# A fused graph layer on one core: VectorE's order between the first and the second group, and three gate matmuls moved

## The reference

```python
h = jnp.maximum(_layernorm(x, axis=-1), 0.0)
# inside the layer, with x standing for h:
c = relu(bn1(conv1d(xc, conv1_w, 0)))                 # 1 tap, along the channels
c = bn2(conv1d(c, conv2_w, 8))                        # 17 taps, along the nodes
x_conv = relu(c + xc)
s = x @ w_se.T + b_se                                 # 3 numbers per node
A = exp(-dist(s, s)) * mask
x_nmp = A @ relu(x @ w_msg.T + b_msg)
gi = concat([x_conv, x_nmp]) @ w_ih.T + b_ih          # gates r, z, n
gh = x @ w_hh.T + b_hh
r, z = sigmoid(gi_r + gh_r), sigmoid(gi_z + gh_z)
nn_ = tanh(gi_n + r * gh_n)
return (1 - z) * nn_ + z * x
```

## Time and profile before

| | |
|---|---|
| median of 3 runs | 283.03 us (282.77 to 283.75) |
| profiled execution | 282.48 us, of which span of the instructions 280.7 us |
| granted TensorE clock, mean | 0.998 |
| PE busy | 273.1 us, 97% |
| DVE busy | 244.4 us, 87% |
| ACT busy | 162.0 us, 58% |
| POOL busy | 63.3 us, 23% |

### The profile page before, as it was taken

The page is one execution under the profiler, slowest core; times in us unless marked ns, Lnnn a source line. Parts: engine busy times, 40 slices in busy tenths (PEclk is TensorE's granted clock), DMA queues, the critical chain, the costliest instruction groups (busy, mean ns, idle before and its releaser), DMA issues.

```text
span 280.7 us, 5274 instructions
## 1 busy us (share of the span) xinstructions
PE 273.1 (97%) x1842; PEld 246.4 (88%) x1842; DVE 244.4 (87%) x550; ACT 162.0 (58%) x270; POOL 63.3 (23%) x125
## 2 busy tenths in 40 slices
PE   7899999999999999999999999999999999999993
PEld 6699977999889988899889998899889998899883
DVE  6899988998999999988999989988999887984656
ACT  3798558737654657526754467536674267542463
POOL 7600020920225002610216002530116100340000
PEclk9999999999999999999999999999999999999999
DMA  7830405656243654182542743263440712043002
GB/s 229 304 43 0 147 6 154 223 117 183 77 152 56 149 198 138 42 132 81 218 152 39 166 152 112 113 95 112 152 152 7 124 54 96 2 61 70 0 0 75
DMA packets 20029, 30.77 MB, mean 110 GB/s; under 512 B 9458, under 2 KB 13876, under 8 KB 19124
## 3 DMA queue, kind: packets, MB, share of 16 engines
q1 hardware_dynamic: 17312, 26.50, 28.6%
q0 software_dynamic: 2544, 3.93, 10.2%
q10 hardware_dynamic: 148, 0.01, 0.0%
HBM read 25.41 MB, written 8.70 MB: 122 GB/s over the span
## 4 chain that ended last, share of the span: by engine, by line
PE 87%; DVE 5%; DMA 2%; ACT 2%; issue 1%; POOL 1%; SPq 0%; DVEq 0%; ACTq 0%; POOLq 0%
PE ps L1311 24%; PE ps L1313 23%; PE ps L1312 23%; PE ps L1364 5%; PE ps L1401 4%; DMA w<-w_conv 2%; PE ps L1424 2%; PE ps L1430 1%; PE ps L1433 1%; PE ps L1391 1%; ACT cp L544 1%; POOL rstd L408 1%; DVE stats L827 1%; DVE n_lo L1031 0%; PE ps L1360 0%
## 5 line engine op out<-in xcount | busy, mean ns | idle before, releaser
L1311 PE MATMUL ps<-v_hi,wt_hi 128*128 128x256 f32 x280 | 79.3, 283 | 0.0
L1313 PE MATMUL ps<-v_hi,wt_lo 128*128 128x256 f32 x280 | 78.8, 282 | 0.0
L1312 PE MATMUL ps<-v_lo,wt_hi 128*128 128x256 f32 x280 | 78.7, 281 | 0.0
L1311 PEld LDWEIGHTS ps<-v_hi,wt_hi 128*128 128x128 f32 x280 | 52.7, 188 | 0.8
L1312 PEld LDWEIGHTS ps<-v_lo,wt_hi 128*128 128x128 f32 x280 | 52.6, 188 | 0.3
L1313 PEld LDWEIGHTS ps<-v_hi,wt_lo 128*128 128x128 f32 x280 | 52.7, 188 | 0.0
L581 ACT ACTIVATE mbs<-ps,par 128x256 f32<-128x256 f32 x24 | 12.0, 501 | 30.7 <-DVE y L970 17.6
L414 POOL TENSOR_TENSOR scale<-vpe,neg_half 128x8 f32<-128x8 f32 x6 | 10.2, 1695 | 83.3 <-DVE scale L844 83.3
L1311 PE MATMUL ps<-h_hi,wt_hi 128*128 128x512 f32 (+1 forms) x67 | 26.7, 398 | 0.5 <-DVE h_lo L879 0.3
L1312 PE MATMUL ps<-h_lo,wt_hi 128*128 128x512 f32 (+1 forms) x67 | 25.7, 384 | 0.0
L1313 PE MATMUL ps<-h_hi,wt_lo 128*128 128x512 f32 (+1 forms) x67 | 25.7, 384 | 0.0
(11 more groups left out here) (167 smaller groups left out, 642.3 us busy)
## 6 DMA issues: line engine op xcount, KB each, us to landing
w<-ln_rows SPq DMA_DIRECT2D x6, 1024.0 KB, 4.7
mask<-adj_t SPq DMA_DIRECT2D x8, 512.0 KB, 3.5
out<-x_t SPq DMA_DIRECT2D x7, 512.0 KB, 5.4
out<-gate POOLq DMA_DIRECT2D x14, 256.0 KB, 4.1
xin<-x_nm SPq DMA_DIRECT2D x6, 512.0 KB, 3.7
xt<-x_t SPq DMA_DIRECT2D x6, 512.0 KB, 4.3
slot_rows<-turned SPq DMA_DIRECT2D x24, 32.0 KB, 3.2
rows<-slot_rows SPq DMA_DIRECT2D x6, 128.0 KB, 3.0
```

Of the source, the lines that this page charges most:

```text
L1311: pe.matmul(dst, wt_hi[:, blk, :], hi, start=start, stop=False)
L1312: pe.matmul(dst, wt_hi[:, blk, :], lo, start=False, stop=False)
L1313: return pe.matmul(dst, wt_lo[:, blk, :], hi, start=False, stop=stop)
```

## The change

On DVE, `ln_stats` takes a range of tiles, and for group 1 it is called twice, for tiles 0 to 3 ahead of the two `n_low` (and now behind `lot_low(12)`) and for tiles 4 to 7 behind them. `update` is cut into `change` (L1074, L1077) and `put_out` (L1081); for group 0, half 0, the two `h_low` of group 1 stand between them. `moments(2)` moves from in front of `level2_b(1, 0)` to behind `v_low_b(1, 1)`. On PE, `gates_xc` is cut into `xc_reset` (three matmuls, reset gate) and `xc_rest` (six), and for group 0, half 1, `xc_reset` stands ahead of `messages(1)`. All other calls give the same instructions in the same order as before. The diff, with the split of `update` left to the words above:

```diff
-            def ln_stats(g):
+            def ln_stats(g, tiles=range(GB)):
 
                 dve.wait_ge(x_landed, 16 * (g + 1))
-                for j in range(GB):
+                for j in tiles:
                     last = stats_of(g, j)
-                last.then_inc(stats_ready, 1)
+                if j == GB - 1:
+                    last.then_inc(stats_ready, 1)
...
             add_shared(0, 1)
-            ln_stats(1)
             lot_low(12)
+            ln_stats(1, range(0, 4))
             n_low(0, 0, 5)
             n_low(0, 1, 7)
+            ln_stats(1, range(4, GB))
             join_y(0, 1, 0)
             join_y(0, 1, 1)
...
             reset(0, 0)
-            update(0, 0)
+            change(0, 0)
             h_low(1, 0)
             h_low(1, 1)
+            put_out(0, 0)
             ln_stats(2)
-            moments(2)
             level2_b(1, 0)
             level2_b(1, 1)
             level1(1)
             v_low_b(1, 0)
             v_low_b(1, 1)
+            moments(2)
             level2_u(1)
...
+            def xc_reset(g, c):
+                pe.wait_ge(xc_lo_ready, NCH * g + c + 1)
+                three(bank(4), IH(R, 0), xc_hi[:, cols(c)], xc_lo[:, cols(c)], False, True).then_inc(r_ps, 1)
...
             conv1(1, 0, 2)
             conv1(1, 1, 7)
+            xc_reset(0, 1)
             messages(1)
-            gates_xc(0, 1)
+            xc_rest(0, 1)
```

More of the change, by code:

```diff
@@ L1069, in slots_low_first, with change @@
                 dve.tensor_tensor(left[:, :, 13], sq[:], left[:, :, 12], ALU.subtract).then_inc(slot_lo, 1)
-            def update(g, c):
+            def change(g, c):
                 dve.wait_ge(cand_ready, NCH * g + c + 1)
@@ L1078, in update, with put_out @@
                                          op1=ALU.mult).then_inc(zd_ready, 1)
+            def put_out(g, c):
                 dve.wait_ge(zd_ready, NCH * g + c + 1)
@@ L1082, in update @@
                                          op1=ALU.add).then_inc(out_ready, 1)
+            def update(g, c):
+                change(g, c)
+                put_out(g, c)
             def part_scaled(p):
@@ L1501, in gates_n, with xc_rest @@
                 three(bank(6), IH(Z, 1), *nm, False, False)
-            def gates_xc(g, c):
+            def xc_reset(g, c):
+                pe.wait_ge(xc_lo_ready, NCH * g + c + 1)
+                three(bank(4), IH(R, 0), xc_hi[:, cols(c)], xc_lo[:, cols(c)], False, True).then_inc(r_ps, 1)
+            def xc_rest(g, c):
                 xc = (xc_hi[:, cols(c)], xc_lo[:, cols(c)])
[L1505 to L1513, removed]
                 if g < NG - 1:
@@ L1519, in gates_xc @@
                     three(bank(5), IH(N, 0), *xc, False, True).then_inc(gin_ps, 1)
+            def gates_xc(g, c):
+                if n_last(g, c):
+                    xc = (xc_hi[:, cols(c)], xc_lo[:, cols(c)])
+                    pe.wait_ge(xc_lo_ready, NCH * g + c + 1)
+                    three(bank(4), IH(R, 0), *xc, False, False)
+                    pe.wait_ge(n_lo_ready, NCH * g + 1)
+                    three(bank(5), IH(N, 0), *xc, True, False)
+                    three(bank(6), IH(Z, 0), *xc, False, False)
+                    return
+                xc_reset(g, c)
+                xc_rest(g, c)
             def part_n_of_h(p):
```

## The result

The changed kernel takes 287.22 us (median of 4 executions, 284.49 to 287.45), the kernel before 283.3 beside it; the ratio is 1.0127, with a 95% interval of 1.0093 to 1.0161. The forecast was 284.7 in a range of 283.3 to 285.9: the direction and the first cause were right, the size was not.

What follows compares the result with a forecast made beforehand. PE was taken as the bound, busy 97% of the span, plus its holes. The early 0.67 us gain is spent waiting for slots: 282.48 + 1.67 = 284.15, plus 0.55 to the median's scale, 284.7 us; range 283.3 to 285.9.

Steps and rivals of the forecast that it cites:

- the first cause: DVE's late moments delays POOL's scale, then distances and the slots; PE's transposes wait, 1.67 us later than before.
- First part: DVE: group 1 statistics in halves about n_low end PE's stall at 35.88; xc still starts at 38.05, worth nothing.
- n stall: PE's short stall at 35.88 for n's low parts, 0.20 us in the timeline, counted as worth 0.45.
- Second and third part: DVE's h_low inside update, PE's reset matmuls before messages: two stalls hidden, first sub-convolution at 51.4, gain 0.67 us.
- The sum: Whole execution: profiled 282.48 us plus 1.67 for late slots gives 284.15, or 284.7 on the median's scale.
- Fourth part: DVE's moments at 50.95 makes POOL's distances 3.07 us later, slots ready at 58.55, PE's transposes 1.67 us later.
- the cap of 0.64: POOL beside DVE's L970: if cover never cost over 0.64 us, slots at 58.15 and time 284.3; judged unlikely.
- no row prices it: TensorE's clock in PE's 2.3 us hole: no earlier PE wait near that long, so no cost was given.
- Rival (d): PE's hole of 2.3 us: equal or more contention, or TensorE's clock lowered; 286 us and above, chance 0.08.
- behind it nothing is late: After PE's wait for slots: rows, exponent, masks and joins move with PE, column-row transfers stay hidden; no further cost.
- The base: Starting time: median of runs 283.03 us, taken as 0.55 above the profiled execution of 282.48.

Runs made afterwards that it cites:

- `reset_only`: Only the reset gate's three xc matmuls moved ahead of messages, against the kernel before: median 283.39 us, ratio 0.998 [0.9937, 1.0023].

## Where the prediction held, and the step that failed

- **First part, right.** The n stall is gone, xc starts at 37.90 (the whole execution lies 0.15 earlier from the start), and the weight load's wait before it has grown from 0.25 to 0.73 (PEld, 37.90 in the profile after); alone this part is worth nothing.
- **Second and third part, right and a little better.** No stall at 45.15 and 47.23. The first sub-convolution comes at 51.00, not 51.4: messages' copies on ScalarE end at 50.94, since messages is not only earlier but also starts with its weight load covered. A gain of 0.92 us (1.07 less the 0.15), against my 0.67. The sum had left it out, rightly: it is spent in the wait for the slots.
- **Fourth part, the mechanism right, the size near by some luck.** Moments at 50.58 (I said 50.95), distances at 53.67 (53.77), slots at 58.86 (58.55), PE 1.88 late (1.67). L414 took 1.97 instead of 1.69, which made up for most of the early moments. I took one operation left when DVE's add_h begins, and 59.15 for two; there were two, L291 and L293, and add_h began 0.31 us earlier than I placed it (56.97, not 57.28). 59.15 less 0.31 is 58.84. The open point, whether POOL can be covered for the whole length of a long DVE operation, is settled by L291, 1.21 us beside L971: the cap of 0.64 is refuted. The Trainium skill ("SBUF — State Buffer", SBUF: two separate sides) has it so, and this trace agrees.
- **The step that failed: the clock's fall stands in the sum as nothing, because "no row prices it".** I had said that PE would stand for 2.3 us where it had no hole. Rival (d) named what could follow, with 0.08 for it and for more contention together, and the sum went on as if the clock held. The runs show it in 8 of the 12 executions of the changed kernel without the transfer wait, at 1.5 us each, and in 8 of the 9 of the changed kernel as it is. It is true that ahead of PE's last matmuls the trace before has no stretch below 1.00, so neither the chance of a fall nor its length could be read there. But I had the rate, half the work per us, and the trace after bears it out: a matmul of 256 columns every 0.22 us against 0.12. With a mean of 0.57 over 4 us, 0.43 of them is lost, 1.7 us, near the 1.5 measured. A state that the trace has never been in needs a term with a range, and a chance to match, not a footnote.
- **A second step failed: "behind it nothing is late".** I followed rows, masks and column rows of the group at hand, and not the same chain in the groups behind. In group 5 the distances of the changed kernel wait 1.31 us for the rows of the slots. In the experiments this wait costs 1.4 us.
- **The base.** I took the median (283.03) as the profiled execution plus 0.55 of no cause. By the experiments it was a mixture: executions near 282.5 and others with a wait of PE in group 5 that the profiled one did not have. SP's chain of stores and loads there was not looked at, since nothing in it was changed. The profiled execution plus 1.9 is 284.4, and that is where the undisturbed executions lie (284.38 to 284.50).

That the transfer wait is there in eight of the nine executions of the changed kernel is read from their times; two profiles show it. Why it goes with the fall of the clock there, and is absent in all ten executions with the filled hole, is open.

## What to carry to other kernels

An instruction moved on one engine moves everything that is queued behind its consumers on other engines: here `moments`, ten small operations, held up eleven of another purpose, which came second in POOL's loop. Before moving a step, read each consumer's queue in program order and ask what stands behind it and how much slack that has (here 0.5 us against 3 us). And where a sum says that a hitherto busy TensorE will stand for two us, give the clock a term of its own. Dummy matmuls in the hole are a remedy while the cause of the hole stays: here it then cost its length and no more.

## What the runs showed of the hardware beyond the forecast

The granted clock fell to its lower level behind holes of 2.69 us and 1.87 us; in other executions it did not behind 1.31, 1.89 or 1.99 us, nor, by their times and mean clocks, in 4 of 12 behind the hole of 2.7 us. The fall behind the hole of 2.7 us cost 1.5 us. POOL operations on 8 and 16 elements a partition that took 0.22 and 0.20 us took 1.21 and 1.10 us beside a DVE operation of 1.22 us on two operands in SBUF; beside operations that read PSUM, POOL's operations took 0.20 to 0.28. In group 5 SP's first load of the rows follows its first store by 7.0 to 7.3 us in the profiled executions with the wait and by 5.0 to 5.4 in those without (7.2 in one with little of it, `reset_only`), with POOL's output transfer issued 0.2 us ahead of the stores in both. By their times about two thirds of the executions of the kernel before have that wait. Holding the output transfers back until the loads had landed took the wait away in all three profiles, and by the times in all 36 executions.
